# Zero-fill copies moved from the POOL queue to the ACT queue, as 2.5 KB rows

## The reference

```python
x = _layernorm(x + L0(x, edges, edge_weight))          # A_w @ (x @ W) + b
x = _layernorm(x + L1(x, edges, edge_type_2))          # two gated relational layers, w = att x basis
x = _layernorm(x + L2(x, edges))                       # degree-normalised convolution
x = _layernorm(x + L3(x, edges, edge_attr_8))          # 8-head attention over the edges
```

```python
logits = einsum('ehd,ehd->eh', q[rows] * scale, k[cols]) + att_bias
p = exp(logits - row_max[rows]); att = p / segment_sum(p, rows)[rows]
y = segment_sum(att[:, :, None] * v[cols], rows)
```

## Time and profile before

| | |
|---|---|
| median of three runs | 1247.96 us |
| the profiled execution | 1259.67 us, of which the span of instructions 1257.9 us |
| TensorE busy | 1181.3 us (94%) |
| VectorE busy | 851.3 us (68%) |
| ACT busy | 437.1 us (35%) |
| POOL busy | 307.6 us (24%) |
| the build | from 66.7 us to about 248 us |
| the 24 zero copies of the build | issued from 72.4 to 208.1 us |
| the scatter | issued from 434.2 to 971.0 us |

### The profile page before, as it was taken

One profiled execution on the slowest core, in us unless ns is written; L12 is line 12 of the kernel. 1 busy time (PEld: TensorE's weight loads), 2 busy tenths in 40 slices (PEclk: granted clock), 3 DMA queues, 4 the chain that ended last, 5 costly groups with the idle time before them and its releaser, 6 DMA issues.

```text
span 1257.9 us, 21464 instructions
## 1 busy us (share of the span) xinstructions
PE 1181.3 (94%) x8083; PEld 540.5 (43%) x8084; DVE 851.3 (68%) x1330; ACT 437.1 (35%) x586; POOL 307.6 (24%) x220
## 2 busy tenths in 40 slices
PE   6987879999999999999999999999999899999997
PEld 2333334323344334345445454455333365555553
DVE  7575657544434555553368875575999889899997
ACT  2444546512122222112311002216553255444454
POOL 2000000000010133344655655545556000000000
PEclk9988989999999999999999999999999899999999
DMA  8567867598799789753122213112223376565653
GB/s 327 209 217 247 297 224 269 151 407 305 243 363 307 257 285 314 278 165 109 2 35 35 50 19 69 2 3 33 34 33 67 139 235 231 202 220 187 213 186 112
DMA packets 64325, 222.73 MB, mean 177 GB/s; under 512 B 31138, under 2 KB 36002, under 8 KB 48272
## 3 DMA queue, kind: packets, MB, share of 16 engines
q1 hardware_dynamic: 34706, 156.38, 35.8%
q0 software_dynamic: 25184, 53.10, 16.7%
q10 hardware_dynamic: 4350, 12.07, 2.8%
HBM read 198.92 MB, written 59.92 MB: 206 GB/s over the span
## 4 chain that ended last, share of the span: by engine, by line
PE 69%; DVE 11%; issue 7%; DMA 7%; ACT 3%; SPq 2%; DVEq 1%; ACTq 0%
PE PS L1853 26%; PE PS L1802 10%; PE PS L1727 6%; PE PS L1657 5%; PE PS L2098 4%; PE PS L2085 4%; DMA R<-R 4%; DVE R L1172 4%; DVE R L1209 4%; PE PS L1675 3%; PE PS L1967 2%; PE PS L2144 2%; PE PS L1889 1%; PE PS L1773 1%; DMA W<-in_basis_s 1%
## 5 line engine op out<-in xcount | busy, mean ns | idle before, releaser
L812 POOL DMA_INDIRECT bias_d<-R x160 | 271.0, 1694 | 331.3 <-DMA bias_d<-R 220.5
L1853 PE MATMUL PS<-R 128*128 128x512 f16 x1300 | 298.1, 381 | 0.0
L1853 PEld LDWEIGHTS PS<-R 128*128 128x128 f16 x1300 | 120.5, 98 | 180.6 <-issue 49.7
L1727 PE MATMUL PS<-R,XX 125*128 125x512 f16 (+2 forms) x612 | 134.7, 354 | 15.3 <-ACT R L1400 6.8
L1613 ACT ACTIVATE R<-PS 128x1024 f32<-128x1024 f32 (+1 forms) x100 | 106.2, 1087 | 109.6 <-PE PS L2085 77.9
L1802 PE MATMUL PS<-W,XX 128*128 128x512 f16 x600 | 136.0, 386 | 5.1 <-DVE R L1010 2.7
L926 DVE TENSOR_SCALAR R<-W,R 125x1250 f16<-125x1250 f16 x160 | 89.4, 606 | 53.7 <-PE PS L1727 39.4
L1172 DVE CUSTOM_DVE_ANT_0 R<-PS,R 128x1250 f16<-128x1250 f32 x80 | 116.8, 1459 | 5.5 <-PE PS L2021 2.9
L2098 PE MATMUL PS<-R 128*32 128x256 f32 (+1 forms) x1600 | 102.5, 391 | 5.2 <-DVE R L1209 5.2
L2085 PE MATMUL PS<-R 128*128 128x256 f16 (+3 forms) x800 | 99.6, 275 | 5.4 <-ACT R L1613 2.2
L779 POOL DMA_DIRECT2D bias_d<-bias_d x39 | 21.6, 556 | 324.0 <-PE PS L1727 164.2
(11 more groups left out here) (231 smaller groups left out, 1411.0 us busy)
## 6 DMA issues: line engine op xcount, KB each, us to landing
bias_d<-bias_d POOLq DMA_DIRECT2D x39, 1280.0 KB, 9.0
R<-in_basis_s SPq DMA_DIRECT2D x32, 1024.0 KB, 6.9
W<-in_basis_s SPq DMA_DIRECT2D x28, 1024.0 KB, 6.1
W<-bias_d SPq DMA_DIRECT2D x27, 1024.0 KB, 4.9
XX<-bias_d SPq DMA_DIRECT2D x13, 1024.0 KB, 4.9
R<-key_d SPq DMA_DIRECT2D x20, 500.0 KB, 4.0
R<-R SPq DMA_DIRECT2D x120, 80.0 KB, 5.9
W<-bias_d SPq DMA_DIRECT2D x7, 904.0 KB, 4.6
```

The source lines that it names most:

```text
L812: pool.indirect_dma_start(bias_d, bass.IndirectOffsetOnAxis(ap=idx[:, c:c + 1], axis=0), attr[:, c, :], None, bounds_check=DUMP + GC * P - ...
L1727: ins = T.matmul(mm_out(3 * (j % 2) + b, p1 - p0), own[0:EC, bass.ds(c, 1), :, :].rearrange("p c m w -> p (c m w)"), hots(p0, p1), start=f ...
L1853: ins = T.matmul(mm_out(SUM_BANK(s, i), D), lhs, rhs, start=n == 0, stop=n == len(terms) - 1)
```

## The change

ACT issues the 24 copies of the build, on its own queue. A copy's access pattern puts the quarter of each row outermost: 4 quarters, then 128 rows, then 640 floats (2560 bytes). Before, the copy's 128 x 10,240 bytes were one contiguous run. A semaphore of their own (`zero_sent`) counts these copies, and POOL waits for both semaphores ahead of the scatter. ACT waits once, ahead of the build, for piece 0. Copy `n` is issued after the same count of `built` as before (ACT's wait for window `w` is `w + 3`). ACT's loop over the 10 blocks is written out, so that line 1400's operand has a fixed address.

```diff
+        cells = bias_d[0:DUMP, :].rearrange("(n p s) h -> n p (s h)", n=ZF, p=P)
@@ gpsimd
-            for n in range(ZB):
-                pool.wait_ge(built, 3 + 4 * ZK * n // ZB)
-                zeros(ZE + n)
@@
-            pool.wait_ge(zero_out, 16 * ZF)
+            pool.wait_ge(zero_out, 16 * (ZF - ZB))
+            pool.wait_ge(zero_sent, 16 * ZB)
@@ scalar
-
-            with act.Fori(0, NT) as t4:
+            act.wait_ge(zero_out, 16 * ZS)
+
+            def zeros(n):
+
+                act.dma_start(cells[n].rearrange("p (b e) -> b p e", e=NN // 2),
+                              cells[0].rearrange("p (b e) -> b p e", e=NN // 2)).then_inc(zero_sent, 16)
+
+            for t4 in range(NT):
                 for j in range(4):
                     act.wait_ge(built, t4 * 4 + (j + 3))
+                    for n in range(ZB):
+                        if 4 * ZK * n // ZB == 4 * t4 + j:
+                            zeros(ZE + n)
                     act.wait_ge(stored[j], t4 * 48 + 48)
                     banks = PS[:, 3 * (j % 2):3 * (j % 2) + 3, :].rearrange("p a b -> p (a b)")
                     S.activation(stage16[:, j, :], banks[:, 0:NN], ACT.Copy).then_inc(copied, 1)
                     act.wait_ge(fixed_up, t4 * 4 + (j + 1))
-                    S.activation(flat(A16[32 * j:32 * j + 32, 1, bass.ds(t4, 1), :]), banks[96:128, 0:NN],
+                    S.activation(A16[32 * j:32 * j + 32, 1, t4, :], banks[96:128, 0:NN],
                                  ACT.Copy).then_inc(evicted, 1)
```

More of the change, by code:

```diff
@@ L331, in gnn_resnorm @@
         zero_out = sem("zero_out")
+        zero_sent = sem("zero_sent")
         own_made = sem("own_made")
@@ L771, in zeros @@
             def zeros(n):
-                cells = bias_d[0:DUMP, :].rearrange("(n p s) h -> n p (s h)", n=ZF, p=P)
                 if n < ZS:
```

## The result

The changed kernel takes 1421.67 us (median of 4 runs, 1419.93 to 1422.54), the kernel before 1249.08 us; the ratio is 1.138, with a 95% interval of 1.136 to 1.141. The profiled execution took 1422.54 us, 162.9 us more than that of before. Forecast: 1435 us, in 1395 to 1495 us.

A forecast was written before the change was run, and what follows sets the result against it. TensorE was taken to bound the build, with copies costing at most about 30 us. A 187 us delay on the profiled 1259.67 us gave 1447 us, less 11.7 us to the median: 1435 us, range 1395 to 1495 us.

The forecast's parts named there:

- The step that decided: On ACT's queue, a transfer uses as many engines as its outermost count splits over, up to 16; count 4 gives 4.
- Rival A: Copies spread over all 16 engines, 3.3 us each, and stores wait less: -17 us, 1231 us; chance 0.10.
- The time of a copy: 1,310,720 bytes over 4 engines at 24.5 GB/s each: 13.4 us a copy, bounds 12.9 and 15.5 us.
- the fast side: Lower bound for one copy's time, allowing 4% more than queue 1's rate: 12.9 us.
- the main sum: After the build, mix 12 waits for a weight store behind piled-up copies until about 454 us: 187 us late.
- the other branch: If the queue can't hold the pile, ACT stands at its issues; build ends near 440, not 248 us: 190 us late.
- one of the prediction's own signs of being wrong: After the build: line 1351's first store landing within 10 us would show the forecast wrong.
- The hardware loop: In ACT's build loop, the register instructions go: 0 to -3 us, counted as nothing in the sum.
- The end of the waits for the stores: In the build, stores no longer stand behind 40 KB packets: 0 to -30 us, counted as nothing.
- The clock after the stall: A slower clock after the long stall costs a few us at most.
- The issue's 0.54 us: ACT's issues of 24 copies, 0.51 us each in the median, 12 us in all; 0 to 12 us on TensorE's path.
- The scatter: The first scatter, at 434.2 us, moves with everything else and finds the copies landed.

The follow-up runs named there:

- e1: The changed kernel with each of ACT's 24 copies as 128 outermost rows of 4 rows of 2560 bytes, so 16 engines: 1242.06 us.
- e2: The changed kernel with each of ACT's 24 copies as 8 outermost rows of 64 rows of 2560 bytes, so 8 engines: 1277.94 us.
- e9: The changed kernel with odd-numbered copies spread over 16 engines and even-numbered ones left on 4: 1316.31 us.
- e5: The changed kernel with copies 0 to 20 over 16 engines, the last 3 on 4 engines and sent at windows 37 to 39: 1282.83 us.
- e7: The kernel before with only ACT's loop over the blocks written out, POOL's copies as before: 1248.52 us.
- e11: e6 again, beside e12 on the same chip: 1237.04 us.
- e12: e1 again, beside e11 on the same chip: 1242.95 us.
- e6: e1 with ACT issuing a window's copy after line 1406 and not ahead of it: 1235.97 us.
- e3: The changed kernel with each of ACT's copies as 4 outermost rows of 8 rows of 40,960 bytes, still 4 engines: 1435.67 us.

## Why the prediction was right

*The engines.* The step that decided, from 8 completions of ACT's stores to 4 engines for the copies, is shown by the packet count, and by e1, e2 and e9, which change only the count of engines. Rival A's condition (16 signals) is not met in the change.

*The time of a copy* was forecast as 13.4 us and is 13.3 by the same kind of row. In the trace a 2560-byte packet of the copies takes 102 ns in the median, 128 of them 13.1 us. But one starts a little before the one ahead of it has ended: from 113 to 119 us, with no stores about, queue 10 moved 247 packets, 4 of them signals, so a row every 99 ns on each of the four engines, and 12.6 us a copy. That is just below the 12.9 us of the fast side.

*The place.* The prediction put the main sum on a pile in the queue, with mix 12 waiting for its store, and gave the other branch beside it: ACT held at its issues. The second happened. The main road failed at its first step, that the queue holds the pile: a held issue came back with some 860 to 1000 rows outstanding, 215 to 250 on each of the four engines, of the 3072 that the 24 copies put on each. So no wait of 180 us for a DMA is seen, and one of the prediction's own signs of being wrong came true: the four stores of line 1350 (1351 before) issued at 421.48 us had all landed by 429.8 us, within 10 us. The mechanism of the first road is real (e5), but had no pile to work on. What saved the number is that the four engines' time is the chain on both roads.

*The size.* The forecast had the delay at 187 to 190 us and it is 162.9. By the second branch's terms: the copies with the build's stores between them took 327.5 us (72.7 to 400.2), not 322 + 23 = 345, as a copy is 12.6 us and not 13.4 (24 of them 302 us); the stores' rows, 222 of them on each engine in that time, are some 22 us, as forecast; the last copy was accepted 28.7 us ahead of the end of all of them, not 13, as the queue holds nearly two copies and not one; and 39 us, not 34, followed until the build's end. That is 410 instead of 438 us.

*The luck in the total.* The delay was forecast 24 us too long, and yet 1435 us is only 13 us above 1421.67. The forecast took 11.7 us off, because the profiled execution before was that much above its median. But what had made it slow was its build (compare e7), which the change replaces: the changed kernel's profiled execution is only 0.9 us above its median. The two errors cancel in part. And the low end of the range is added up wrongly: 12.9 us a copy (12 us less) and half of the loads (15 us less) make a delay of 160 us and not 150.

*The parts counted as nothing.* The hardware loop: nothing, by e7. The end of the waits for the stores: line 631's stores land in 2.7 us in the median (5.9 before), and it wins nothing in the change, as said. The clock after the stall: nothing, as the time from the end of the build on is the same. The issue's 0.54 us: 6 us where it is not hidden (e11 and e12), within the 0 to 12. The scatter moved with everything else, and found the copies landed.

*Rival A's price* was too high. It gave 1231 us; e1, which is its case, takes 1242. The 30 us that the copies "cost at most" were read from one execution whose stores had waited long (18.3 us, against 6.3 in e7's). Against the median of before, A brings 5 to 7 us; its best form, e6, 11 to 12.

## What to carry to other kernels

Before a copy is cut into short rows, look at the outermost count that this leaves: on ACT's hardware queue counts of 4, 8 and 128 gave 4, 8 and 16 DMA engines, and the count of completion packets in the profile's table of queues tells it. With 128 outermost, 2.5 KB rows cost nothing by themselves and let small, urgent transfers through. And a transfer that no one waits for still costs the engine that issues it, once its queue is full: the chain of waits then names the issue, not the transfer.

## What the runs showed of the hardware that I had not expected

ACT's hardware queue holds few rows. With 4 engines a held issue ended when some 860 to 1000 rows were outstanding (the change), with 8 engines when 1060 to 1200 were, 133 to 150 an engine (e2's longer issues, up to 5.8 us). It is not a limit of bytes: in e3 up to 107 pieces of 40 KB, 3.3 copies, were outstanding, and no issue took over 0.69 us. A full queue of one engine's DMAs left the other's alone: SP's issues of line 631 stayed at 592 ns while ACT stood for 8 us.

Two queues on one DMA engine took turns piece by piece. These are the two hardware queues of e3 from 135 to 143 us, when only the four engines had work:

```profile
q10 hardware_dynamic: 24, 0.82, 23.7%
q1 hardware_dynamic: 24, 0.04, 1.3%
```

24 packets of either: in the trace, on each engine, every 40 KB piece of a copy (1.5 us) is followed by one row or one signal of a store. A copy has 8 pieces and a signal on an engine, and a window's three stores have 6 rows and 3 signals, 9 against 9. So one window's stores get through with each copy, some 12.5 us, and this is the turn of line 1406 in e3. With four windows' stores in the queue the last rows land as late as 48.3 us after their issue, though the median of 2.6 us doesn't show it. A turn costs a store little when the pieces are short: with 2.5 KB rows the same stores landed in 2.7 us in the median and 5.3 us at most, though the four engines were full. The Trainium skill (DMA: Bandwidth & Descriptors, section on queues, rings and completion order) says that an engine drains a packet of about 9 to 17 descriptors (single reads or writes, not the packets that the profile counts) before it changes rings. e3 does not show that: it has one at a time.
